# A convolution and mixture-of-experts block on one core: results of the last two bands scattered to their tokens, and an end without beats

## The reference

```python
# step 1: involution (a convolution whose kernels are made from the pixel), 7x7, 16 groups of 8 channels
xn  = layer_norm(x)                                   # over channels
r   = relu((xn @ w_reduce - mean) * (gamma / sqrt(var + 1e-3)) + beta)    # 32 features
kg  = (r @ w_span + b_span).reshape(B, H, W, 16, 49)
x   = x + sum over the 49 taps of kg[..., g, k] * shifted(xn)[..., g, c]
# step 2: mixture of experts, 8 experts, each token goes to its two best
t   = x as 12544 tokens of 128
tn  = layer_norm(t)
p   = softmax(tn @ gate_w + gate_b);  two largest p and their experts
t   = t + sum over the two experts e of p_e * (gelu(tn @ W1[e] + b1[e]) @ W2[e] + b2[e])
```

## Time and profile before

| what | us |
|---|---|
| runs timed | 1445.42, 1455.03, 1455.09 |
| their median | 1455.03 |
| the profiled execution, its own time | 1449.3 |
| its span, first to last instruction | 1447.5 |
| mean granted TensorE clock, share of full | 0.754 |

### The profile page before, as it was taken

How to read it: one execution, slowest core, us unless ns; L and a number is a source line. 1 busy time by engine, 2 the same in 40 slices (tenths; PEclk the granted TensorE clock), 3 DMA queues, 4 the chain that set the end, 5 groups by cost and what they waited for, 6 DMA issues and landing times.

```text
span 1447.5 us, 29676 instructions
## 1 busy us (share of the span) xinstructions
PE 960.6 (66%) x11249; PEld 838.2 (58%) x11249; DVE 497.3 (34%) x1612; ACT 553.9 (38%) x1198; POOL 488.6 (34%) x536
## 2 busy tenths in 40 slices
PE   2687764888197792877928878379694687726540
PEld 1576653687096680876817768268583576725440
DVE  6111230345043450344513444123442235413432
ACT  5244330666054460453614545135351333312220
POOL 3000144012604517035171351712516136254425
PEclk9586665899598785897868778679876787656785
DMA  5659613463154532545425363252631422212322
GB/s 135 138 111 270 134 46 75 90 156 79 48 144 104 117 98 68 123 105 127 99 73 128 88 143 93 75 120 59 138 91 53 100 63 68 76 49 77 96 62 63
DMA packets 184078, 144.04 MB, mean 100 GB/s; under 512 B 65110, under 2 KB 169558, under 8 KB 183488
## 3 DMA queue, kind: packets, MB, share of 16 engines
q1 hardware_dynamic: 168114, 115.03, 33.2%
q0 software_dynamic: 14336, 25.72, 6.7%
q10 hardware_dynamic: 1486, 1.38, 0.4%
HBM read 89.70 MB, written 52.36 MB: 98 GB/s over the span
## 4 chain that ended last, share of the span: by engine, by line
PE 39%; issue 21%; another core or an unknown queue 10%; SPq 7%; ACT 7%; DVE 7%; POOL 3%; DVEq 2%; DMA 1%; ACTq 1%; POOLq 0%
PE e L1182 11%; PE kg L1148 9%; PE hy L1252 5%; PE hy L1262 5%; SPq L365 3%; POOL got L583 2%; PE back L1194 2%; ACT kb L662 2%; PE misc L1215 2%; DVEq L975 2%; ACT tn L677 2%; PE hy L1243 2%; SPq L431 1%; PE misc L1207 1%
## 5 line engine op out<-in xcount | busy, mean ns | idle before, releaser
L662 ACT ACTIVATE kb<-kg 112x896 f32<-112x896 f32 x224 | 205.6, 918 | 451.4 <-PE kg L1148 363.7
L1182 PE MATMUL e<-kb,win 112*32 112x64 f32 x6272 | 241.8, 291 | 182.3 <-issue 165.2
L583 POOL DMA_INDIRECT got<-yrows,pos x224 | 215.9, 964 | 331.9 <-DMA yrows<-yo 141.0
L1148 PE MATMUL kg<-rT,wk 98*112 98x112 f32 x1792 | 270.9, 313 | 75.5 <-ACT kb L662 42.2
L1182 PEld LDWEIGHTS e<-kb,win 112*32 112x32 f32 x6272 | 185.4, 131 | 230.1 <-issue 209.5
L569 POOL DMA_INDIRECT xrows<-tn,pos x224 | 213.8, 954 | 285.0 <-DVE pos L955 151.9
L1148 PEld LDWEIGHTS kg<-rT,wk 98*112 98x112 f32 x1792 | 233.9, 206 | 102.6 <-ACT kb L662 54.3
L712 ACT ACTIVATE hT<-hy,staged 128x128 f32<-128x128 f32 x490 | 152.6, 364 | 287.1 <-PE hy L1252 181.6
L1262 PE MATMUL hy<-staged,hT 128*128 128x128 f32 x980 | 179.7, 313 | 51.1 <-issue 22.3
L825 DVE TENSOR_TENSOR conv<-e,group_mask 128x448 f32<-128x448 f32 x112 | 69.7, 622 | 387.2 <-PE e L1182 258.4
L1252 PE MATMUL hy<-xT,staged 128*128 128x128 f32 x980 | 186.5, 321 | 19.1 <-issue 11.9
(11 more groups left out here) (113 smaller groups left out, 602.3 us busy)
## 6 DMA issues: line engine op xcount, KB each, us to landing
win<-xpad SPq DMA_DIRECT2D x56, 784.0 KB
xin<-xrows SPq DMA_DIRECT2D x56, 256.0 KB
yrows<-yo SPq DMA_DIRECT2D x56, 256.0 KB
t_row<-in_x_dram SPq DMA_DIRECT2D x64, 112.0 KB
xpad<-xs SPq DMA_DIRECT2D x240, 28.0 KB
out_dram<-t_row SPq DMA_DIRECT2D x56, 112.0 KB
xs<-in_x_dram SPq DMA_DIRECT2D x48, 112.0 KB
xrows<-tn SPq DMA_DIRECT2D x4, 896.0 KB, 14.6
```

Of the source, the lines that this page charges most:

```text
L583: pool.indirect_dma_start(got[:, slot * C:(slot + 1) * C], None, yrows[n % 2], bass.IndirectOffsetOnAxis(ap=pos[n % 2][:, k * COLS + c:k * ...
L662: act.activation(kb[:, lo:lo + 8 * PATCHES].rearrange("p (h k) -> p h k", h=2), kg[0:WIN, :].rearrange("p (h k) -> p h k", h=2)[:, :, 0:4 ...
L1148: mm = pe.matmul(kg_bank[j % 2][0:WIN, i * PATCHES:(i + 1) * PATCHES], wk[:, at:at + WIN], r[:, :, :, b4 + i], start=True, stop=True, skip ...
L1182: mm = pe.matmul(to, w[:, at:at + 32], rhs, start=True, stop=True, skip_group_check=True)
```

## The change

1. For bands 5 and 6 (`n >= LATE`, LATE = 5) each row in DRAM carries one more number: rows of `placed_rows` have 129 floats (CR1), the last of which is the place to which the result of the row goes in a new table `yback`. `tn` and `xin` get 129 columns per row throughout. Padding rows have a place of their own behind the real ones.
2. Setting up those tables once, in band 1: at beat 30 SP issues two DMAs that write zeros to both tables (4480 rows of 516 bytes each), at beat 46 two that write the own places of the rows (4480 single numbers each, 516 bytes apart). Three more iotas on POOL at the start.
3. `scatter` of bands 5 and 6: before each eight columns POOL copies eight places into column 129 of `tn`; the DMAs move 516 bytes per row. One more small instruction and wait in `positions`.
4. Results of bands 5 and 6: POOL issues one indirect DMA for each tile (`send_back`), 128 rows from `yo` straight to the token's place in `yback`, as soon as `put_y` of the tile is done. `store_rows` and `gather` of these bands are gone. DVE takes the places out of `xin` once for each group (`take_place`). `yback` is read by eight plain DMAs a band (`load_back`, four columns each), and `mix_piece` adds four columns per piece.
5. The loop ends at beat 458 (LAST = 459). Behind it the visits left (`tail_visits`: 20 to 35 of band 5, all 36 of band 6) stand without beats between them. On POOL the 30 scatters that are left stand three and three, with one `send_back` of band 5 behind each three, ten in all; the other `send_back`s follow. Band 5's pieces are loaded and mixed in visits 12 to 30 of band 6.
6. In the last band ten tiles are staged ahead (AHEAD) in place of three: six in the `win` tiles, which the convolution no longer needs. All ten `stage`s stand in DVE's last visit of band 5, behind `put_y` of its last tile.
7. `store_out` waits strip by strip for these two bands; the scatter semaphore is split in four.

```diff
+    LATE = NC - 2
+    LAST = BEATS * NC + 11
+    AHEAD = 10
...
             def load_rows(n, g):
...
-                sp.dma_start(xin[k % 2][:, 0:have * C].rearrange("p (i c) -> p i c", c=C),
-                             xrows[n % 2][4 * g * 128:(4 * g + have) * 128, :].rearrange("(i p) c -> p i c", p=128)) \
+                rows, width = (placed_rows, CR1) if n >= LATE else (xrows, C)
+                sp.dma_start(xin[k % 2][:, 0:have * CR1].rearrange("p (i c) -> p i c", c=CR1)[:, :, 0:width],
+                             rows[n % 2][4 * g * 128:(4 * g + have) * 128, :].rearrange("(i p) c -> p i c", p=128)) \
...
+            def load_back(n, piece):
+                if piece == 0:
+                    for odd in range(2):
+                        sp.wait_ge(y_sent[odd], sent(last_group(n, odd)))
+                if n == LATE:
+                    sp.wait_ge(mixed, mixed_by(LATE - 1) + max(0, piece - 1))
+                else:
+                    sp.wait_ge(mixed, mixed_by(LATE))
+                    sp.wait_ge(main_done, STEPS * NC)
+                s, k = divmod(piece, 2)
+                rows = yback[((n - LATE) * 2 + k) * T * COLS:((n - LATE) * 2 + k + 1) * T * COLS, :]
+                sp.dma_start(got_at(n, piece), rows.rearrange("(p q) c -> p (q c)", p=T)[:, 4 * s * C:4 * (s + 1) * C]) \
+                    .then_inc(got_last[piece] if n == NC - 1 else got_back[piece % 2], 16)
+            def zero_places():
...
+                    sp.dma_start(placed_rows[i].rearrange("(p k) c -> p k c", p=T),
+                                 got_zeros.unsqueeze(1).to_broadcast([T, XROWS // T, CR1])).then_inc(places_zero, 16)
+            def mark_places():
...
+                        sp.dma_start(placed_rows[i].rearrange("(p k) c -> p k c", p=T)[:, :, C],
+                                     own_rows[:, i * (XROWS // T):(i + 1) * (XROWS // T)]).then_inc(places_marked, 16)
...
             def scatter(n, i):
...
+                if n >= LATE and i % 8 == 0:
+                    hf = q % 2
+                    if q >= 2:
+                        pool.wait_ge(scattered[q - 2], 16 * 8 * (n + 1))
...
+                    pool.tensor_copy(tn[:, :].rearrange("p (c e) -> p c e", e=CR1)[:, 8 * hf:8 * hf + 8, C],
+                                     place_f[:, k * COLS + 8 * hf:k * COLS + 8 * hf + 8]).then_inc(placed, 1)
...
+            def send_back(n, i):
+                g = GROUPS * n + i // 4
+                pool.wait_ge(y_out, NT * n + i + 1)
+                pool.indirect_dma_start(yback, bass.IndirectOffsetOnAxis(ap=place[g % 3][:, i % 4:i % 4 + 1], axis=0),
+                                        yo[g % 2][:, (i % 4) * C:(i % 4 + 1) * C], None).then_inc(y_sent[g % 2], 16)
...
-            for beat in range(BEATS * (NC + 2)):
+            for beat in range(LAST):
...
-                if 0 <= n - 2 < NC:
+                if 0 <= n - 2 < LATE:
                     for i in rows_moved(o, GATHER):
                         gather(n - 2, i)
+                if visit(beat):
+                    m, i = visit(beat)
+                    if m == LATE and i:
+                        send_back(m, i - 1)
...
+            rest = [i for o in range(LAST - BEATS * NC, SCATTER[1]) for i in rows_moved(o, SCATTER)]
+            results = [(m, i - 1) for m, i in tail_visits() if i]
+            for k, i in enumerate(rest):
+                scatter(NC - 1, i)
+                if k % 3 == 2 and results[k // 3][0] == LATE:
+                    send_back(*results[k // 3])
+            mingled = sum(1 for k in range(len(rest)) if k % 3 == 2 and results[k // 3][0] == LATE)
+            for m, i in results[mingled:]:
+                send_back(m, i)
...
             def expert_visit(n, i):
+                ahead = AHEAD - 1 if n == NC - 1 else 3
                 if i:
                     put_y(n, i - 1)
-                    if i + 3 < NT:
-                        stage(n, i + 3)
-                if i >= SLOTS - 4 and n + 1 < NC:
+                    if i + ahead < NT:
+                        stage(n, i + ahead)
+                if i >= SLOTS - 4 and n + 1 < NC - 1:
                     stage(n + 1, i - SLOTS + 4)
+                if i == SLOTS - 1 and n == LATE:
+                    for k in range(AHEAD):
+                        stage(NC - 1, k)
...
+            for m, i in tail_visits():
+                expert_visit(m, i)
+                if m == NC - 1 and 16 <= i < 32 and i % 2 == 0:
+                    mix_piece(LATE, (i - 16) // 2)
+            for piece in range(8):
+                mix_piece(NC - 1, piece)
```

More of the change, by code:

```diff
@@ L179, in metaformer_kernel @@
         te = [sb(f"te{i}", [1, NT], I32) for i in range(2)]
-        xin = [sb(f"xin{i}", [128, 4 * C]) for i in range(2)]
+        xin = [sb(f"xin{i}", [128, 4 * CR1]) for i in range(2)]
+        place_base = sb("place_base", [T, 2 * COLS])
+        place_f = sb("place_f", [T, 2 * COLS])
+        place = [sb(f"place{i}", [128, 4], U32) for i in range(3)]
         xT = sb("xT", [128, 4 * 128])
@@ L409, in load_rows @@
                 if g == 0:
-                    sp.wait_ge(scattered, 16 * 2 * COLS * (n + 1))
+                    for i in range(4):
+                        sp.wait_ge(scattered[i], 16 * 8 * (n + 1))
                 if k >= 2:
@@ L472, in _ @@
                 put_xn(u, (1,))
-            for beat in range(BEATS * (NC + 2) + 3):
+            for beat in range(LAST):
                 n, o = divmod(beat, BEATS)
@@ L1051, in _ @@
             moments1(3)
-            for beat in range(BEATS * (NC + 3)):
+            for beat in range(LAST):
                 n, o = divmod(beat, BEATS)
@@ L1181, in apply @@
                     at = (b * PW + pw) * 64 + (q % 2) * 32
[L1182 removed]
+                    mm = pe.matmul(to, w[0:WIN, at:at + 32], rhs, start=True, stop=True, skip_group_check=True)
                 if pw == PW - 1:
```

162 lines of the change are left out of this document (138 added, 24 removed).

## The result

The changed kernel takes 1462.03 us (median of 7 runs, 1456.5 to 1466.0), the kernel before beside it on the same chip 1451.48 (7 runs): a ratio of 1.0068 with a 95% interval of 1.0039 to 1.0097. It is slower by some 10 us. I had forecast 7.5 us faster.

A forecast was written before the change was run, and what follows sets the result against it. No engine is full; the core nearly stands while POOL issues indirect DMAs back to back. Terms +6 +10 +14 -12 -25.5 = -7.5 took 1449.3 to 1441.8 us, 1447 forecast for the median, range 1412 to 1488.

The forecast's parts named there:

- What bounds the kernel: Whole kernel: no engine full, others nearly stand while POOL issues indirect DMAs back to back; 0.72 us per gather, up to 1.4 per scatter.
- Band 1, setting up: Band 1: zeros on SP's queue make `xin` 6 us late, marks taken as nothing; +6 us, bounds 0 and +15.
- Band 5 in the loop: Beats 425 to 458: 19 added sends, 11 among band 4's gathers; +10 us, bounds 0 and 27.
- Scatter to first result: Band 6's first scatter to its first result: more indirect DMAs, ten stages ahead; 62.7 becomes 77, +14 us, bounds 68 and 95.
- Band 6's experts: Band 6's first to last result: band 5's gathers gone, DVE sets the pace; 79.9 becomes 68, -12 us, bounds 60 and 85.
- The end: Behind the last result: last send, eight mixed pieces and store replace 32 gathers; 50.5 becomes 25, -25.5 us, bounds 22 and 30.
- The set-up is the change's cost: Rival, band 1: zeros and places hold SP's queue 30 us or more; +10 to +20, around 1468; chance 0.08.
- Lone sends cost nothing: Rival, loop and last bands: a send alone behind its result is free; -35 us, 1420; chance 0.33.
- Each send costs what a gather costs: Rival, all sends: each indirect DMA holds the others, burst or not; +38 at 1.0 us each, 1493; chance 0.20.

The follow-up runs named there:

- e8: Kernel before, each scatter of bands 0 to 5 waiting for ACT's kernel copy of its own beat; ratio 0.9469 to the kernel before.
- e9: e6 with each scatter of bands 0 to 5 also waiting for ACT's kernel copy of its own beat; ratio 0.9328 to the kernel before.
- e1: Kernel before plus the change's zeros and marks in band 1, into tables nobody reads; ratio 1.0214 to the kernel before.
- e3: Kernel before plus the marks alone (4-byte pieces, band 1's beat 46), into tables nobody reads; ratio 1.0123 to the kernel before.
- e4: Kernel before plus 19 sends at the places of band 5's sends in the loop, to a table nobody reads; ratio 1.0143 to the kernel before.
- e11: Kernel before plus only 12 of e4's 19 sends, all among band 4's gathers; ratio 1.0145 to the kernel before.
- e5: Kernel before plus 54 lone sends in beats of six bands without other indirect DMAs, to a table nobody reads; ratio 1.0010 to the kernel before.
- e2: Kernel before plus the zeros alone (516-byte rows, band 1's beat 30), into tables nobody reads; ratio 1.0189 to the kernel before.
- e16: e2 with table rows of 512 bytes in place of 516; ratio 1.0017 to the kernel before.
- e6: Changed kernel, zeros in 3612-byte pieces at band 1's beat 9 and marks at beat 10, beneath band 0's scatters; ratio 0.9873 to the kernel before.
- e12: e9 with every second scatter of bands 0 to 5 also waiting for the landing of the one ahead; ratio 0.9973 to the kernel before.
- e7: Kernel before, each scatter of a band waiting until the one ahead of it has landed; ratio 1.0954 to the kernel before.

## Why the prediction was wrong, step by step

**What bounds the kernel.** That the core nearly stands while POOL issues without a pause was right, and e8 and e9 show the missing pause as a cause. But I priced an indirect DMA by kind (scatter 1.4, gather 0.72, lone send 0.25) where the price goes by whether POOL pauses in between.

**Band 1, setting up: the step that failed.** Forecast +6 with an upper bound of 15 and 10 for the marks; measured +30 (e1) to +35. The term was mis-sized at each half. The zeros I took at 23 us by bytes or 26 by packets at the mean of 46 ns; they took 36.6 to land, since a packet of 516 bytes takes 74. That alone would be 10 us over the 26. The rest is the order of the queue: I let `xin` land behind the zeros at once, but SP, held by its own issues, sent it off at 271 and was done with it at 292; PE waited 20.0 us, not 6. The marks I called free because the windows behind them were for later; the next `xin` load (327.3, 7.3 us on SP) and behind it a store of `yo` (334.6) also stood behind them, DVE waited 10.9 us for that store, and they cost 10 (e3). Had this term been +30, the same sum would have given +16.5. The sentences on the Trainium skill pointed to the right place: a row off a boundary costs more. The estimate of 34 us for the zeros was near the 36.6. With the 11 us that it added the term would have been 17 and the total +3.5, where 30 to 35 and +11.1 were measured: SP's held queue and the marks are not in it.

**Band 5 in the loop.** Forecast +10, measured +19.1 here and +17.8 with the sends alone (e4). The bounds held. I had 8 us for 11 among gathers and 2 for 8 alone; it is 17 for 12 and nothing for the 7 behind them (e11).

**Scatter to first result.** +14 against +12.0; in other runs with the change 76.8 to 78.4 us in place of 74.7. The sum hit (its parts add up to 76.3, not the 76.5 that I wrote), its parts did not all. POOL issued 30 DMAs without a pause (1307.7 to 1345.5) where I had it wait a little, and the ten stages took 9.3 us from band 5's last result to band 6's first, not 12.5. POOL's timeline at the end of that run:

```profile
1344.60 0.94 POOL L689 DMA_INDIRECT placed_rows<-tn,pos  x1 [0.30 <-issue]
1350.60 1.09 POOL L696 DMA_INDIRECT yback<-yo,place  x1 [5.06 <-DVE yo L1154]
```

**Band 6's experts.** -12 against -23.0, below my lower bound: 56.9 us, where I had summed 60 of DVE's work and 7 for sends. The misreading is in the earlier trace rows itself: in the 33.0 us of 23 results DVE was busy 15.63 (PE 28.37), so 1.45 us was not DVE's load; that it is the time of a turn through PE, ACT and DVE is my reading, and no run varies it. After the change results still come 1.45 us apart at first (1382.4, 1383.9, 1385.3, 1386.8), and 34 x 1.45 = 49. The other 8 us come mostly where a piece of band 5 is mixed: from the 16th result on each second interval is 2.5 to 2.7 us. The clock was 0.97, as in the stretch without gathers and not as in the one with them. The sends wait for their results and hold nobody that the intervals show:

```profile
1389.14 0.96 POOL L696 DMA_INDIRECT yback<-yo,place  x1 [0.30 <-issue]
1390.72 0.96 POOL L696 DMA_INDIRECT yback<-yo,place  x1 [0.62 <-DVE yo L1154]
1392.91 1.09 POOL L696 DMA_INDIRECT yback<-yo,place  x1 [1.23 <-DVE yo L1154]
```

**The end.** -25.5 against -31.2; 19.3 us, below the lower bound of 22:

```profile
1440.53 0.95 POOL L696 DMA_INDIRECT yback<-yo,place  x1 [0.30 <-issue]
1442.77 2.67 SPq L488 DMA_DIRECT2D win<-yback  x6
...
1445.79 2.39 DVE L1182 SCALAR_TENSOR_TENSOR t_row<-win,wt,t_row 112x128 f32<-112x128 f32 x8 [6.47 <-DMA win<-yback]
1448.20 8.42 SPq L457 DMA_DIRECT2D out_dram<-t_row  x8
...
1453.44 2.38 DVE L1182 SCALAR_TENSOR_TENSOR t_row<-got,wt,t_row 112x128 f32<-112x128 f32 x8
```

The first mix came 6.5 us behind the last result (I had 7.7), the mixes took 10.0 (11), and only 2.8 us of the store stood behind the last (6.4), as it goes out strip by strip beside the mixes.

**The rivals.** "The set-up is the change's cost" named the cause and, at 1468, nearly the time; I gave it 0.08. "Lone sends cost nothing" was right of its mechanism (e5, and the last band) and wrong of the time, as it had no price for the twelve among gathers. "Each send costs what a gather costs" fell with e5. That the total still came out inside the range owes something to luck: against a set-up 29 us and a loop 9 us dearer than put, the experts and the end together were 17 us cheaper.

## What to carry to other kernels

Price a transfer by the shape of its descriptors and by what stands behind it on its queue, not by its bytes: the same zeros cost 20 us as single rows of 516 bytes, and as rows of 512 or in pieces of 3612 nothing that stands clear of the noise. Where POOL issues many indirect DMAs, look whether it ever waits between them, and if another engine's progress is at hand as a semaphore, pace it by that; then check that the last one still lands before its reader is due. A result interval is an engine's load only if that engine is busy all through it.

## What the runs showed of the hardware that was not expected

- Zeros written by SP in single rows of 516 bytes took a DMA engine 65 ns a row (e2; 74 in the changed kernel) where rows of 512 took 29 (e16), and while they were written all 16 engines together moved 135 GB/s (changed kernel, 262 to 278 us; e16: 271). Rows of 516 bytes that were read took 32 ns, and seven of them in one packet of a scatter 187 ns.
- 8960 pieces of 4 bytes, 30 ns each in the changed kernel, cost 10 us where an `xin` load and a store of `yo` are due behind them (e3), and nothing beneath the scatters (e6).
- Scatters issued in one run of 32 cost the kernel copies beside them 1.17 us each, in runs of 3 to 12 0.65 (e8), in pairs or singles with pauses of 1.6 to 9 us between them about 0.2 (e12, e7; estimates from band 1 against band 0). What in the chip holds the other engines' semaphores meanwhile, no run shows.
